# Cross-attention and quantised FFN on one core: the normalised x and its f16 high part both computed on ACT

## The reference

```python
x_n = (x - mean(x)) / sqrt(var(x) + 1e-5)               # rows of 512
q, k = ctx @ Wq.T + bq, ctx @ Wk.T + bk
attention = softmax(q @ k.T)                            # 512 x 512
x = x + einsum('bln,bmn->blm', x_n, attention)
```

## Time and profile before

| | |
|---|---|
| median of 3 runs | 289.44 us (287.11 to 290.83) |
| the profiled execution: time | 287.0 us |
| its span, first to last instruction | 285.2 us |
| mean granted clock of PE | 0.938 |
| busy: PE, DVE, ACT, POOL | 229.8, 252.3, 169.1, 81.6 us |

### The profile page before, as it was taken

How to read it: one execution, slowest core, us unless ns; L and a number is a source line. 1 busy time by engine, 2 the same in 40 slices (tenths; PEclk the granted TensorE clock), 3 DMA queues, 4 the chain that set the end, 5 groups by cost and what they waited for, 6 DMA issues and landing times.

```text
span 285.2 us, 3245 instructions
## 1 busy us (share of the span) xinstructions
PE 229.8 (81%) x937; PEld 99.1 (35%) x946; DVE 252.3 (88%) x369; ACT 169.1 (59%) x287; POOL 81.6 (29%) x104
## 2 busy tenths in 40 slices
PE   7867559987984099707699798999999989999972
PEld 7423214433431043202344243344444434444320
DVE  2489999999987999999979999699999999899940
ACT  2257136468994276856875999855556555665200
POOL 1067200022005300053420501932312333444453
PEclk9997968999999579766999999999999999999999
DMA  4968999999999635687340228355554376744651
GB/s 150 384 240 180 268 230 195 278 260 237 258 133 283 117 74 137 122 153 148 70 92 18 43 53 129 90 129 130 130 128 77 80 163 133 173 90 97 166 126 58
DMA packets 103077, 42.92 MB, mean 150 GB/s; under 512 B 93844, under 2 KB 96152, under 8 KB 102552
## 3 DMA queue, kind: packets, MB, share of 16 engines
q1 hardware_dynamic: 100224, 35.93, 58.0%
q10 hardware_dynamic: 2360, 6.83, 7.4%
q0 software_dynamic: 480, 0.02, 0.1%
HBM read 15.48 MB, written 4.19 MB: 69 GB/s over the span
## 4 chain that ended last, share of the span: by engine, by line
DVE 50%; PE 15%; ACT 13%; issue 8%; POOL 6%; DMA 5%; SPq 1%; POOLq 0%; ACTq 0%; DVEq 0%
DVE amax L751 13%; PE ps L699 6%; DVE w_int L794 5%; PE ps L711 4%; DVE vw L937 3%; DVE hq L942 3%; DVE pf L858 3%; DVE stats L894 3%; PE ps L654 3%; DMA wst<-in_L_ffn_W 3%; DVE wquant L848 3%; DVE phl L918 2%; DVE nmax L904 2%; DVE xhl L930 2%; ACT phl L558 2%
## 5 line engine op out<-in xcount | busy, mean ns | idle before, releaser
L654 PE MATMUL ps<-pT,xT 128*128 128x512 f16 x192 | 50.0, 416 | 13.6 <-DMA pT<-phl 10.4
L699 PE MATMUL ps<-w1T,cxT 128*128 128x512 bf16 x256 | 58.0, 380 | 0.0
L711 PE MATMUL ps<-w2T,xhl 128*128 128x512 bf16 x247 | 56.7, 379 | 1.6 <-issue 1.0
L554 ACT ACTIVATE wst<-ps 128x1024 bf16<-128x1024 f32 x32 | 32.4, 1020 | 25.6 <-PE ps L699 25.6
L751 DVE TENSOR_REDUCE amax<-phl 128x64 f32<-128x2048 bf16 x16 | 36.5, 2280 | 4.3 <-ACT phl L558 4.3
L654 PEld LDWEIGHTS ps<-pT,xT 128*128 128x128 f16 x192 | 20.0, 106 | 47.7 <-issue 31.6
L642 PE MATMUL ps<-qkT 128*128 128x512 f32 x32 | 18.5, 684 | 21.5 <-ACT pf L453 17.4
L419 POOL TENSOR_TENSOR wst<-wst,vs 128x512 bf16<-128x512 bf16 x16 | 18.5, 1158 | 60.4 <-DVE wquant L853 30.8
L711 PEld LDWEIGHTS ps<-w2T,xhl 128*128 128x128 bf16 x256 | 23.7, 98 | 30.8 <-issue 3.6
L699 PEld LDWEIGHTS ps<-w1T,cxT 128*128 128x128 bf16 x256 | 23.7, 98 | 30.1 <-issue 3.6
L558 ACT ACTIVATE phl<-wst 128x2048 bf16<-128x2048 bf16 x16 | 30.6, 1910 | 1.3
(11 more groups left out here) (77 smaller groups left out, 366.1 us busy)
## 6 DMA issues: line engine op xcount, KB each, us to landing
wst<-in_L_ffn_W ACTq DMA_DIRECT2D x6, 1024.0 KB, 5.8
xs<-in_x SPq DMA_DIRECT2D x4, 1024.0 KB, 8.1
out_x<-wst SPq DMA_DIRECT2D x16, 256.0 KB, 2.8
cx<-in_ctx SPq DMA_DIRECT2D x4, 512.0 KB, 5.4
wst<-in_L_ffn_W SPq DMA_DIRECT2D x2, 1024.0 KB, 9.6
xhl<-pf SPq DMA_TRANSPOSE x17, 4.3
xT<-xhl SPq DMA_TRANSPOSE x16, 4.4
pT<-phl SPq DMA_TRANSPOSE x16, 3.5
```

The lines of the kernel that those rows point to most:

```text
L554: act.activation(ys[:, k, 1024 * g:1024 * g + 1024], ps_y[:, 2 * g:2 * g + 2, :], ACT.Copy)\
L654: pe.matmul(ps_pv[:, t % 2, :], xT[:, t, NT * a + n, :], pT[:, :, NT * c + n, :], start=(s == 0), stop=False)
L699: last = pe.matmul(ps_y[:, c, :], h1T[:, k, t, :], w1T[:, 4 * c:4 * c + 4, t, :], start=False, stop=(t == KT - 1))
L711: last = pe.matmul(ps_z[:, k, :], h2T[:, k, t, :], w2T[:, t, :], start=False, stop=(t == FT - 1))
```

## The change

The two activations of a tile, `x_high` and the new ACT function `normalise`, both read x itself and apply scale rx and bias offx = -mean * rx. DVE's `normalise` is gone; DVE keeps the subtraction `x_low`, which now waits for both activations. POOL computes offx with two more instructions for each batch. The line numbers of the changed kernel are larger than those of the kernel before by 2 to 15.

```diff
--- before.py
+++ after.py
@@ -95,6 +95,8 @@
         ms = sb("ms", [P, LT], F32)
         rs = sb("rs", [P, 3, LT, 2], F32)
         rx = sb("rx", [P, LT], F32)
+        mx = sb("mx", [P, LT], F32)
+        offx = sb("offx", [P, LT], F32)
         off = sb("off", [P, LT], F32)
         squares = sb("squares", [P, 2, H], BF16)
         half = sb("half", [P, LT], F32)
@@ -166,7 +168,7 @@
         rsr = [sem(f"rsr{n}") for n in range(3)]
         nm, off_rdy = sem("nm"), sem("off_rdy")
         v_mean, v_mean2, v_ms = sem("v_mean"), sem("v_mean2"), sem("v_ms")
-        rx_rdy = sem("rx_rdy")
+        rx_rdy, mx_rdy, offx_rdy = sem("rx_rdy"), sem("mx_rdy"), sem("offx_rdy")
 
         xT_rdy = [sem(f"xT_rdy{t}") for t in range(LT)]
         pT_rdy = [sem(f"pT_rdy{t}") for t in range(NT)]
@@ -348,9 +350,13 @@
                 wait_alone(pool, mvr, LT * (b + 1), pool_gate)
                 wait_alone(pool, xn_rdy, LT * b, pool_gate)
                 pool.tensor_scalar(rs[:, 0, :, 0], mv[:, :, 1], EPS, None, ALU.add).then_inc(ve[0], 1)
+                pool.tensor_scalar(mx[:, :], mv[:, :, 0], -1.0, None, ALU.mult).then_inc(mx_rdy, 1)
                 rsqrt(0, b)
                 wait_alone(pool, rsr[0], b + 1, pool_gate)
                 pool.tensor_scalar(rx[:, :], rs[:, 0, :, 1], XSCALE, None, ALU.mult).then_inc(rx_rdy, 1)
+                wait_alone(pool, mx_rdy, b + 1, pool_gate)
+                wait_alone(pool, rx_rdy, b + 1, pool_gate)
+                pool.tensor_tensor(offx[:, :], mx[:, :], rx[:, :], ALU.mult).then_inc(offx_rdy, 1)
 
             def mean_x1(b):
                 wait_alone(pool, x1_rdy, LT * (b + 1), pool_gate)
@@ -460,9 +466,16 @@
                    .then_inc(p_hi, 1)
 
             def x_high(b, t):
-                act.wait_ge(xn_rdy, b * LT + (t + 1))
+                if t == 0:
+                    act.wait_ge(offx_rdy, b + 1)
                 wait(act, xT_rdy[t], 16 * b)
-                act.activation(xhl[:, t, 0, :], xn[:, t % 2, :], ACT.Copy).then_inc(x_hi, 1)
+                act.activation(xhl[:, t, 0, :], xs[:, LT * b + t, :], ACT.Identity, scale=rx[:, t:t + 1],
+                               bias=offx[:, t:t + 1]).then_inc(x_hi, 1)
+
+            def normalise(b, t):
+                wait(act, x_lo, b * LT + (t - 1))
+                act.activation(xn[:, t % 2, :], xs[:, LT * b + t, :], ACT.Identity, scale=rx[:, t:t + 1],
+                               bias=offx[:, t:t + 1]).then_inc(xn_rdy, 1)
 
             def load_w1(u):
                 act.wait_ge(w_step[W1], W_STEPS * (u - 1) + 5)
@@ -514,6 +527,8 @@
                         x_high(front, t)
                     if t > 0:
                         p_high(front, t - 1)
+                    if t < NT:
+                        normalise(front, t)
                     if b is not None and t > 1:
                         x_plus(b, t - 2)
                     if t == 2 and b is not None:
@@ -918,15 +933,9 @@
                 dve.scalar_tensor_tensor(phl[:, t, 1, :], pf[:, t, :], rinv[:, t, 1:2], phl[:, t, 0, :],
                                          ALU.mult, ALU.subtract).then_inc(p_lo, 1)
 
-            def normalise(b, t):
-                if t == 0:
-                    dve.wait_ge(rx_rdy, b + 1)
-                wait_alone(dve, x_lo, b * LT + (t - 1), dve_gate)
-                dve.tensor_scalar(xn[:, t % 2, :], xs[:, LT * b + t, :], mv[:, t, 0:1], rx[:, t:t + 1],
-                                  ALU.subtract, ALU.mult).then_inc(xn_rdy, 1)
-
             def x_low(b, t):
                 dve.wait_ge(x_hi, b * LT + (t + 1))
+                dve.wait_ge(xn_rdy, b * LT + (t + 1))
                 dve.tensor_tensor(xhl[:, t, 1, :], xn[:, t % 2, :], xhl[:, t, 0, :], ALU.subtract)\
                    .then_inc(x_lo, 1)
 
@@ -948,12 +957,10 @@
 
 
                 negmax(b, 0)
-                normalise(b, 0)
                 if w1 is not None:
                     w_amax(W1, w1)
 
                 negmax(b, 1)
-                normalise(b, 1)
                 recip(b, 0)
                 if w1 is not None:
                     w_power(W1, w1)
@@ -967,7 +974,6 @@
                     h1_amax(h1)
 
                 negmax(b, 2)
-                normalise(b, 2)
                 recip(b, 1)
                 if h1 is not None:
                     h1_power(h1)
@@ -982,7 +988,6 @@
                     w_over(W2, w2)
 
                 negmax(b, 3)
-                normalise(b, 3)
                 recip(b, 2)
                 if h1 is not None:
                     h1_over(h1)
```

## The result

The change makes the kernel slower by 0.6%: 290.16 us against 288.70 us (medians of 20 runs each), ratio 1.006, interval 1.0041 to 1.0079, or +1.2 to +2.3 us. I had forecast +2.8 us, and 292.2 us for the time. The direction is right and so are most of the places; the size is 1.6 times too large. The profiled execution of the changed kernel took 289.99 us, 3.0 us more than that of before, which is close to my sum of 2.8. So the sum describes the two profiles, and what has to be explained is why the medians lie closer together.

The account below looks back on a forecast made before the run. ACT was taken to bound fronts 0 and 2, PE to hold back front 1's gain, DVE to bound front 3. Terms 2.6 + 0 + 1.4 + 0.6 (POOL) - 1.8 = +2.8 on 289.4 gave 292.2 us, range 286.5 to 296.5.

Parts of the forecast that it names:

- my sum of 2.8: Whole kernel: the terms of the four fronts and POOL together make it 2.8 us slower.
- the term of front 0 (+2.6): Front 0: ACT is late, so the last x_low moves from 26.66 to 29.25 us, +2.6 us.
- ACT's chain of 10.4 us: Front 0: ACT's work from x_high of tile 0 at 18.76 until the last normalise ends at 29.20, 10.44 us.
- a fall of PE's clock: Sign of being wrong: PE's clock falls in a stretch where it was full; nothing in the sum allows for it.
- Front 1: Front 1: DVE gains 1.84 us but loses it waiting 1.1 us for PE's energies of batch 2; term 0.
- Front 2: Front 2: ACT is the bound, 2.82 us more work less 1.38 of vanished waits; last x_low at 84.0, term +1.4.
- POOL: Ahead of times_w: two more POOL instructions delay factors_v(0), on which DVE waits; +0.6 us.
- Front 3: Front 3: DVE is the bound, waits for nobody and gains 1.84 us.
- Rival B: All fronts: ACT bounds every front, also 1 and 3; +6.3 us, 295.7 us; chance 0.16.
- Rival A: All fronts: DVE bounds them and ACT hides its new work; all 7.4 us come back, 282.0 us; chance 0.14.
- Rival C: Fronts 1 and 2: front 1's gain isn't lost to PE, ACT enters front 2 at about +0.8; 290.4 us; chance 0.20.

Follow-up runs that it names:

- e2: The kernel before with ACT normalising in front 0 alone, DVE in fronts 1 to 3; ratio to before 1.0117, about +3.4 us.
- e6: The changed kernel with 3 and 6 idle products on PE ahead of the energies of tiles 2 and 3 of batch 0; ratio to before 1.0083.
- e1: The kernel before, unchanged, run and profiled a second time; ratio to before 1.002.
- e10: The kernel before with factors_x(3) moved behind factors_v(0) and mean_x1(1) on POOL; ratio to before 0.9947, -1.5 us.
- e4: The kernel before with ACT normalising in fronts 1 and 3, DVE in fronts 0 and 2; ratio to before 0.9968, -0.9 us.
- e9: The kernel before with the change's two POOL instructions for each batch (mx and offx), read by nothing; ratio to before 1.0076.
- e3: The kernel before with ACT normalising in front 2 alone; ratio to before 1.0051, +1.5 us.
- e5: The kernel before with 3 and 6 idle products on PE ahead of the energies of tiles 2 and 3 of batch 0; ratio to before 0.9962, -1.1 us.
- e8: The changed kernel without the normalise activation, x_low subtracting the high part from x itself; ratio to before 0.9966, -1.0 us.
- e7: As e5, with idle products also after the transposes of contexts 1 and 2 and the queries and keys of batch 1; ratio to before 0.9959.
- e11: The kernel before with ACT normalising in fronts 1 and 3, e5's idle products and e10's POOL order; 283.36 us, ratio to before 0.9811.
- e12: As e11, but with ACT normalising in front 3 alone; ratio to before 0.9863.

## Why the prediction was right or wrong

**What failed is the size of the term of front 0 (+2.6), as far as the profiles show it, and through it the sum.** I set ACT's chain of 10.4 us against a last `x_low` at 26.66, and took that row as what the kernel before does. It is what it does when PE keeps its clock. The chain itself was right: from the last `bn_aggr` to the last `x_low` the changed kernel takes 13.36 us against 10.72, +2.64 for a forecast 2.6, and 13.35 in e2 and e6. But before takes 11.65 in e1, and the kernels with the same front 0 and no idle products took 11.50, 11.65 and 11.83 (e10, e4, e9) and once 10.74 (e3). Against the 11.65 that is usual the term is 1.7, and the sum 1.9, within the measured +1.2 to +2.3. The row that could have told me stood in my own group: a window clock of 0.89 at the front says that the clock was no settled thing there, and the median 2.4 us above the profile said that this execution wasn't the usual one. I carried that difference over to the changed kernel as a constant, and there it is 0.2 us. Of the 2.0 us by which 292.2 is too high, 0.7 is the median of three runs (289.44, where 20 runs give 288.70) and 1.3 the cost of the change.

That this term is the whole of the error is argued, not shown, and e2 speaks against it: front 0 alone on ACT cost 2.5 to 4.2 us, not 1.7. In its profile front 1 is 2.0 us longer as well, and in that of e6 2.3 us, while in the changed kernel's own it is 0.6 shorter. So the parts, measured one by one, don't add up to the whole, and what a late front 0 costs in front 1 stays open. I had also named a fall of PE's clock as a sign of being wrong. It came, 0.63 for 0.89 in front 0, and cost nothing there: ACT's copy of the context starts at 25.11 without a wait, PE's transposes for it end at 24.33.

Front 1: DVE's gain of 1.84 was forecast as lost to PE, in a wait of 1.1 us ahead of front 2. The stretch went from 26.26 to 25.67, 0.6 shorter, so two thirds were lost. The place was another: DVE waits 0.61 us for the energies of tile 3 inside front 1, which stand behind values(0, 0) on PE, and not at all ahead of front 2. The size isn't fixed either. These are values(0, 0) in the changed kernel and in e6, the same program but for the idle products:

```profile
43.78 4.06 PE L669 MATMUL ps<-pT,xT 128*128 128x512 f16 x12 [0.48 <-DMA pT<-phl]
```

```profile
46.18 5.28 PE L669 MATMUL ps<-pT,xT 128*128 128x512 f16 x12 [1.86 <-DMA pT<-phl]
```

From the first row maximum of front 1 to the end of values(0, 0) it is 8.2 us in the one and 10.8 in the other, DVE's wait behind it is 0.61 and 3.52 us, and the stretch 25.67 and 28.58. With DVE's `normalise` in front 1 the stretch is DVE's own 26.25 us in five profiles of nine, without a wait; in the four others (26.95 to 28.57) and in all five without it (25.67 to 28.58) DVE waits for PE. In these nine it is 17.5 to 18.2 us from the end of values(0, 0) to the first row maximum of front 2. So PE does hold back what DVE gains, and how much depends on when the transposes of the weights come: issuing the four of batch 0 holds SP for 9.73 us in before, 9.77 in the changed kernel, 11.27 in e2 and 12.00 in e6. Why they take longer in some executions stays open.

Front 2: forecast +1.4 for ACT over what it inherits; the last `x_low` was at 83.45 for 84.0. The stretch is 1.75 us longer in the changed kernel and 1.05 in e3. For fronts 1 and 2 together I had +1.4 and the profile has -0.6 and +1.75: the two misses nearly cancel, so that the profiles meet the sum is in part luck.

POOL: 0.6 forecast, 0.8 measured (11.14 for 10.31; e9 the same). That this is close is in part luck. offx took 0.89 us in that place, above my bound of 0.7, beside DVE's p_low; but before, the instruction in that place was `ms` of factors_v(0), which took 0.83 us there and takes 0.19 now, and ahead of the power of factors_v(0) a wait of 0.5 us has come in.

Front 3: forecast -1.84, measured -1.82 (17.71 for 19.53), in every kernel with ACT in front 3. Rival B falls with that: DVE waits for nobody in this front. What followed moved as a block: the first product of W1 starts at 140.7 for 138.2, and between there and the end the profile is about 0.5 us longer (147.5 for 147.0). That is no effect of the change: over the fourteen profiles this part takes 146.9 to 148.9 us, 147.9 in e5, which is the kernel before with idle products, and 147.0 in e6, the changed kernel with them. One set of products of W1 that takes 5.31 us in place of 3.63 stands there in the changed kernel, and one in e5 as well.

Rival A (0.14) is out by e8. Rival C, a smaller inheritance in front 2, gave 290.4 and so came nearest to the measured number, but by luck: it has front 2 begin about 0.8 us later, and in the profile it begins 1.7 us later (65.34 for 63.66).

## What to carry to other kernels

Work moved from the busiest engine to a less busy one pays where the receiving engine has time at that place: cut the profile into the program's own stages and compare the new work with the receiver's idle time in each, then move it only there (here front 3, with a gain of 1.8 us, where moving all four lost 1.7). An absolute row of one execution is a term only if the kernel does that every time; take a second profile of the kernel before when its runs spread over more than the effect forecast, and look first at a granted clock below full in a stretch whose engine others wait for. A wait shown as the receiver's own can also be a queue order: three small POOL instructions moved behind others gave 1.5 us, about what the whole change cost.

## What was unexpected of the hardware

In two executions of one program PE kept its upper clock after pauses of 0.80 and 1.32 us between short bursts and fell to the lower after pauses of 1.42 and 1.32 (1.12 and 2.08 us for the same two products). Nine idle products of together 2.3 us held it in the profiles of e5, e6, e7 and e11, but not in that of e12; in the kernel before they were worth 1.1 us (0.2 to 2.0). A POOL instruction on 128x4 values took 0.19 or 0.20 us with DVE idle or on a reduction, and 0.83 to 0.89 us beside a three-operand instruction of DVE, whichever POOL instruction stood in that place (`ms` in before, offx in the changed kernel, rx in e10).
